# Second batch's masks bank by bank, its scores ahead of two products with values, and two VectorE operations exchanged, in a decoder layer on one core

## The reference

```
qh = (q @ Wq + bq); kh = (k @ Wk + bk); vh = (v @ Wv + bv)
scores = einsum('bhqd,bhkd->bhqk', qh, kh) * scale
scores = where(causal, -inf, scores)
attn = softmax(scores, axis=-1)
out = einsum('bhqk,bhkd->bhqd', attn, vh) @ Wo + bo
```

## Time and profile before

| | us |
|---|---|
| median of 3 runs | 371.53 |
| lowest and highest | 370.04, 372.04 |
| the profiled execution | 369.38 |
| its span, first to last instruction | 367.6 |
| TensorE busy | 338.3 |
| VectorE busy | 254.6 |
| ScalarE busy | 238.9 |
| GpSimd busy | 163.5 |

### The profile page before, as it was taken

How to read it: one execution, slowest core, us unless ns; L and a number is a source line. 1 busy time by engine, 2 the same in 40 slices (tenths; PEclk the granted TensorE clock), 3 DMA queues, 4 the chain that set the end, 5 groups by cost and what they waited for, 6 DMA issues and landing times.

```text
span 367.6 us, 8998 instructions
## 1 busy us (share of the span) xinstructions
PE 338.3 (92%) x3283; PEld 280.1 (76%) x3299; DVE 254.6 (69%) x555; ACT 238.9 (65%) x586; POOL 163.5 (44%) x148
## 2 busy tenths in 40 slices
PE   7878679999999999999999999999999998989697
PEld 3657457987789877987789867987789866858596
DVE  5674786677766976677775976678765966482974
ACT  4552663776756866677847766677848764787551
POOL 4237150364615366363625457362634550445340
PEclk9999999999999999999999999999999999999999
DMA  5940102022031400413023400404014300013300
GB/s 151 307 172 1 31 2 107 37 62 85 1 112 78 144 0 17 171 33 110 0 66 120 143 0 14 169 7 137 0 47 141 116 6 10 30 16 116 116 29 30
DMA packets 22314, 26.97 MB, mean 73 GB/s; under 512 B 2896, under 2 KB 20112, under 8 KB 22288
## 3 DMA queue, kind: packets, MB, share of 16 engines
q1 hardware_dynamic: 21472, 26.52, 22.3%
q10 hardware_dynamic: 816, 0.10, 0.2%
HBM read 24.51 MB, written 2.10 MB: 72 GB/s over the span
## 4 chain that ended last, share of the span: by engine, by line
PE 77%; DVE 9%; issue 7%; ACT 4%; POOL 1%; DMA 1%; ACTq 0%; DVEq 0%; POOLq 0%
PE c L1208 22%; PE a L1208 16%; PE b L1208 14%; PE b1k L1344 7%; PE b1k L1208 6%; PE b2k L1208 4%; DVE negmax L912 2%; PE c L1371 2%; ACT prob L596 1%; ACT probT L558 1%; PE a L1223 1%; DVE scD L893 1%; PE b2k L1223 1%; DMA wk_c<-in_L_attn_Wk 1%; PE a L1301 1%
## 5 line engine op out<-in xcount | busy, mean ns | idle before, releaser
L460 POOL TENSOR_TENSOR w_lo<-w_in,w_hi 128x512 fp32r<-128x512 f32 x32 | 40.8, 1305 | 30.4 <-ACT w_hi L558 26.3
L596 ACT ACTIVATE prob<-b,negmax 128x128 f32<-128x128 f32 x124 | 36.1, 398 | 25.4 <-DVE negmax L912 25.4
L1344 PE MATMUL b1k<-ident,prob 128*128 128x128 f32 x256 | 40.0, 279 | 9.3 <-ACT probT L558 4.5
L466 POOL TENSOR_TENSOR w_lo<-w_in,w_hi 128x512 fp32r<-128x512 f32 x28 | 35.5, 1287 | 28.6 <-ACT w_hi L558 26.8
L453 POOL TENSOR_TENSOR rstA<-varA,minus_half 128x16 f32<-128x16 f32 x8 | 23.4, 2927 | 49.2 <-DVE varA L1047 49.2
L1344 PEld LDWEIGHTS b1k<-ident,prob 128*128 128x128 f32 x256 | 28.1, 140 | 17.3 <-ACT prob L596 7.2
L558 ACT ACTIVATE w_hi<-w_in 128x512 fp32r<-128x512 f32 x64 | 39.1, 653 | 2.6 <-PE b L1208 2.6
L1208 PE MATMUL c<-xTC_hi,w_hi 128*128 128x256 f32 x108 | 31.8, 294 | 0.8 <-DVE xTC_lo L862 0.8
L919 DVE COPY probT<-b1k 128x512 f32<-128x512 f32 x32 | 22.0, 687 | 13.1 <-PE b1k L1344 13.0
L1208 PE MATMUL c<-w_hi,h_hi 128*128 128x256 f32 x96 | 30.8, 321 | 0.1
L1208 PE MATMUL c<-xTC_lo,w_hi 128*128 128x256 f32 x108 | 30.5, 282 | 0.0
(11 more groups left out here) (301 smaller groups left out, 1110.4 us busy)
## 6 DMA issues: line engine op xcount, KB each, us to landing
w_in<-in_L_ffn_w SPq DMA_DIRECT2D x16, 1024.0 KB, 5.6
x_in<-in_x SPq DMA_DIRECT2D x8, 256.0 KB, 2.8
c_in<-in_ctx SPq DMA_DIRECT2D x8, 256.0 KB, 2.9
out<-x2b SPq DMA_DIRECT2D x7, 256.0 KB, 2.2
b_cur<-in_L_ffn_b SPq DMA_DIRECT2D x8, 128.0 KB, 3.0
W_sb<-in_L_attn_W SPq DMA_DIRECT2D x2, 256.0 KB, 4.2
decay_sb<-in_decay SPq DMA_DIRECT2D x1, 512.0 KB, 3.8
h_in<-in_L_xattn_Wk SPq DMA_DIRECT2D x1, 256.0 KB, 4.3
```

Of the source, the lines that this page charges most:

```text
L460: pool.tensor_tensor(w1_lo[:, :, part], w1_in[:, :, part], w1_hi[:, :, part].bitcast(F32), ALU.subtract).then_inc(s_w1lo, 1)
L466: pool.tensor_tensor(w2_lo[:, part, :], w2_in[:, part, :], w2_hi[:, part, :].bitcast(F32), ALU.subtract).then_inc(s_w2lo, 1)
L596: ins = nc.scalar.activation(prob[:, u % PR, g, :], score_banks[u][:, g * P:(g + 1) * P], ACT.Exp, bias=negmax[:, u, g:g + 1], scale=-1.0)
L1344: ins = nc.tensor.transpose(b1k[:, g * P:(g + 1) * P], prob[:, u % PR, g, :], ident[:, :])
```

## The change

In steps 1 to 7 TensorE gives the masks of batch 1 in the order in which their banks come free, with a wait for each (exp of unit 0, 1, 2, 3), instead of one wait for all four; scores(1) stands ahead of values 0 and 1 instead of behind them. VectorE does maxima 5 before the copy of unit 3. Step 8 has its own order and keeps it, and there the masks and the wait stay as they were.

```diff
@@ VectorE
                 if do_b:
                     maxima(4)
+                    maxima(5)
                     probT_odd(3)
-                    maxima(5)
@@ TensorE, scores(bk)
-                    elif do_a:
-                        pe.wait_ge(s_prob, 8 * b + PR)
-                    else:
+                    elif not do_a:
                         pe.wait_ge(s_attTlo, b)
                         pe.wait_ge(s_x2, b)
                         pe.wait_ge(s_prob, 8 * b + 2)
-                    for bank in banks:
-                        mm(bank[:, :], ident_bf[:, :], mask_bf[:, :, :].rearrange("p g m -> p (g m)"),
+                    first = (2, 3, 0, 1) if bk == 1 and do_a else range(PR)
+                    for n, r in enumerate(first):
+                        if bk == 1 and do_a:
+                            pe.wait_ge(s_prob, 8 * b + n + 1)
+                        mm(banks[r][:, :], ident_bf[:, :], mask_bf[:, :, :].rearrange("p g m -> p (g m)"),
                            start=True, stop=False)
@@ TensorE, order
                 if do_b:
+                    scores(1)
                     with_values(0)
                     with_values(1)
-                if do_b:
-                    scores(1)
                 if do_c:
                     down(4)
```

## The result

| | before | after |
|---|---|---|
| median of 4 runs each | 370.8 | 366.73 |
| lowest and highest | 370.04, 372.04 | 365.43, 367.76 |
| the profiled execution | 369.38 | 367.76 |
| its span | 367.6 | 366.0 |
| one loop step | 41.80 | 40.98 |

The ratio is 0.9894, with a 95% interval of 0.9861 to 0.9927: 4.1 us or 1.1% faster. The spans of the two profiles differ by only 1.6 us, although six steps are each 0.8 shorter. The page shows why: TensorE's granted clock, which stood at 9 in every slice before, has three slices at 8 early in the span and one near its end (the last but one).

What follows compares the result with a forecast made beforehand. TensorE, busy 40.84 of 41.80 us per loop step, plus its stand-stills was taken as the bound. Order 0.14 plus wait 0.60 make 0.74, times six steps 4.4, so 371.53 becomes 367.1; range 365.0 to 370.0, forecast's own 365.0 to 368.2.

Steps and rivals of the forecast that it cites:

- first score product: On TensorE in a loop step: scores move ahead of values 0 and 1, starting 0.70 us earlier, 171.62 instead of 172.32.
- down(4) and T(3): On TensorE: down product 4 and transposes of unit 3, behind the reordered work, start 0.14 us earlier.
- T(5): Transposes of unit 5 on TensorE: start 0.74 us earlier per loop step, 0.14 from order and 0.60 from the wait.
- whole step: The whole loop step: 0.74 us shorter, about 41.06 instead of 41.80, if later joints move too.
- TensorE's order: Masks, scores, then values on TensorE: three array shape changes instead of four, 3.04 us instead of 3.18, saving 0.14.
- The wait of exp(3): Last mask on TensorE waits for unit 3's exponentials, ending 171.09; mask due 171.31, weights some 0.2 before: just ready.
- rival 3: Late exponentials of unit 3 hold TensorE; every 0.1 us costs 0.1; one unit late gives 373.4, slower; chance 0.07.
- Max(5) in front of copy(3): On VectorE: maxima 5 run in idle time before unit 3's copy, cost it nothing; it starts 0.14 us earlier.
- Step 1: First pipeline pass: gains nothing, length unchanged; maxima 4 follow the statistics without idle; transposes of unit 4 at most 0.61 later.
- Rivals 1 and 2: First: added waits or new joint pay part back, 368.5 to 370.0, chance 0.15; second: VectorE binds, 371.5, chance 0.12.
- Rival 2: At retention's output product: VectorE's outT comes no earlier, so nothing is left, 371.5, no change; chance 0.12.
- The sum: Over six steps: 6 x 0.74 = 4.4 us gained, median 371.53 to 367.1; chance of gain 3.4 to 5, 0.66.

Runs made afterwards that it cites:

- e2: The changed kernel again with no edit, beside the kernel before: 366.34 us, ratio 0.9886.
- e4: Kernel before with TensorE's part alone (masks bank by bank, scores ahead of values 0 and 1), VectorE's order as before: 370.34 us, ratio 0.9976.
- e5: Changed kernel with masks of batch 1 in unit order behind one wait for the exponentials of unit 3 instead of four waits: 369.07 us, ratio 0.9946.
- e3: Kernel before with VectorE's exchange alone, maxima 5 ahead of the copy of unit 3: 367.27 us, ratio 0.9904.
- e7: Changed kernel with TensorE's idle time in steps 1 and 9 filled with products of zeros: 364.40 us, ratio 0.9816.
- e8: Kernel before with TensorE's idle time in steps 1 and 9 filled with products of zeros: 369.38 us, ratio 0.9954.
- e6: Changed kernel with scores back behind values 0 and 1 and VectorE's exchange undone, leaving mask order and four waits: one run, 372.1 us.

## Why the prediction was right

The forecast of 367.1 was 0.4 above the median of 366.73 (0.8 above the 366.34 of e2), and each link of its chain is in the trace. Against T(2), in a loop step:

| | forecast | measured |
|---|---|---|
| first score product | 0.70 earlier | 172.32 - 170.22 = 2.10 to 171.97 - 170.54 = 1.43: 0.67 |
| down(4) and T(3) | 0.14 | 3.18 to 3.08: 0.10 |
| T(4) | 0.14 | 5.48 to 5.37: 0.11 |
| T(5) | 0.74 | 7.64 to 6.99: 0.65 |
| whole step | 0.74 | 41.80 to 40.98: 0.82 |

- **TensorE's order.** The joint that no row had, scores straight to W, measures 173.04 - 171.97 = 1.07, exactly that of S(0) to retention, and W to down(4) 0.58. The missing 0.04 is nearly all in the start of the masks (0.36 to the first weight load, about 0.47 to the first mask, where 0.43 was taken; e4's trace, which has that mask's record, shows 0.47). The order with one change of shape less is worth 0.10, and e4's loop step keeps 0.07. That it is the change of shape that pays follows from counting the joints; no run changes the shape alone.
- **The wait of exp(3).** It ends 170.16 + 1.26 = 171.42, and the last mask's weights load at 171.47, noted as released by it; the mask itself comes in its place. "Just ready" was right to 0.05, and e5 shows what it would be not to be: rival 3's mechanism is real, and the order of the banks is what keeps it away. It was given 0.07; its price had been 0.1 for each 0.1, and e5 pays 0.45 for a first mask 0.48 later.
- **Max(5) in front of copy(3)** carries nearly all of it (e3). The prediction's steps contained this but did not say it: its chain began with the scores that come earlier, and these alone are worth next to nothing (e4). Its own rows allowed the split: 0.63 of idle before copy 3 holds one maxima's 0.60 even when maxima 4 doesn't move. So here the number was right and the weight that the text gave to its two parts was not.
- **T(5)** came 0.09 less early than forecast: 0.03 from the order and 0.06 from the transposes of retention to T(5), 0.49 instead of the 0.43 taken from another pair.
- **A gain that the prediction left out:** T(7). Before, it waited for copy(6) on ScalarE, without an idle note, since the modelled end of the transposes before it covered it:
```profile
182.23 0.69 ACT L558 ACTIVATE probT<-b1k 128x512 f32<-128x512 f32 x1
```
```profile
182.36 0.66 PE L1223 MATMUL a<-ident,xnA 128*128 128x128 f32 x4
182.98 0.66 PE L1344 MATMUL b1k<-ident,prob 128*128 128x128 f32 x4
```
and after:
```profile
181.97 0.66 PE L1223 MATMUL a<-ident,xnA 128*128 128x128 f32 x4
182.47 0.65 PE L1345 MATMUL b1k<-ident,prob 128*128 128x128 f32 x4
```
ScalarE's copy(6) is 0.80 earlier against T(2), TensorE in front of T(7) only 0.71, and the pair takes 0.50 instead of 0.62: 0.12 per step. e3 has 0.49 there and e4 0.62, so this too comes with VectorE's exchange. With the 0.65 at T(5) and 0.05 between T(5) and the retention output product (1.59 instead of 1.64) that makes the 0.82.
- **Step 1** gains nothing, as forecast. At full clock, in e7 and e8, the retention output product starts 10.44 behind retention in both, 54.23 - 43.79 and 54.43 - 43.99. With the changed order of VectorE T(4) waits there for copy 3 and comes 0.11 later against retention (7.21 instead of 7.10); VectorE is last at the product all the same, as e7's TensorE shows:
```profile
43.79 1.08 PE L1208 MATMUL a<-scD,vA 128*32 128x128 f32 x32 [0.17 <-DVE scD L893]
...
54.23 1.99 PE L1208 MATMUL a<-W_sb,outT 128*128 128x256 f32 x8 [0.56 <-DVE outT L1127]
```
- **Rivals 1 and 2** did not come: the waits cost 0.02 (e6), and outT kept ahead of its product by the same 0.13 (178.12 + 0.87 = 178.99, product 179.12). Rival 2 made its case hang on maxima 4 coming earlier; in e3 maxima 4 does not move, and 0.72 is won all the same.
- **The sum.** 4.4 forecast; 4.98 at equal clock. Per step 0.74 was forecast and 0.82 measured. That the first comparison shows 4.1 and not 5.0 is put down to the clock: its medians, of four runs each, mix executions with different numbers of stretches at the lower level. The prediction took the 2.15 between the profile of before and its median as a fixed distance; it is this mixture, 369.3 at 1.000 against 370.2, 371.8 and 372.4 at the others. That the forecast of the median came within 0.4 is in part luck: the sum was 0.6 short, and the mixture took 0.2 back (371.53 - 4.98 would be 366.55, measured 366.73).

## What to carry to other kernels

Before moving work on the busiest engine, look whether a queue beside it holds an operation that is ready behind one that is waiting: here one exchange of two VectorE operations gave nearly nine tenths of the gain (0.72 of 0.82 per step), paid from 0.63 us of idle time. Work moved ahead of other work on an in-order queue needs its wait split by resource and ordered by when each is free; with a single wait, half of the gain was lost here (0.45 of 0.82). Profiles of two kernels are to be compared step by step at equal granted clock, not by their spans.

## What the runs showed of the hardware

The same program runs with TensorE's mean granted clock at 1.000, 0.995, 0.991 or 0.986, different from one execution to the next, with median spans of 367.5, 368.4, 370.0 and 370.5 us (the kernel before, 66 runs). Where the profiles of the unfilled kernels show the lower level, it comes behind idle time of TensorE. Twenty-three products of zeros in idle time, 5.0 us of TensorE work in all, made the runs of each kernel agree within 0.3 us and both kernels faster: 371.79, the median of the kernel before in the same comparison, to 369.38, and 366.34 of e2 to 364.40. The filling thus removes the lower clock, but idle time is not all that it takes, as the kernel before kept full clock in its first profile with the same idle time. Why an execution falls at one place and not at another is open; nothing was run on it.
